# Two mixture stages: from all experts on all tokens to gathered rows of the chosen pairs

## The chip, the cores and the metric

The program runs on one core of one Trainium2 chip. The metric is the device time of one execution in microseconds (us), as the median of the runs. One execution was profiled; its rows are what the text argues from.

## The reference, cut to what matters

The program is six blocks on 4096 tokens of 256 numbers: a feed-forward block with 8 experts, an attention, that feed-forward block again, then a mixture block (stage d), a second attention (stage e) and the mixture block again (stage f). Only d and f are touched. Each computes

```python
scores = softmax(xt @ gate_w.T)          # 4096 x 16, xt is the normalised input
# only 2 of the 4 groups of 4 experts stay, and of what stays the best 4 experts
c = c.at[arange(T)[:, None], indices].add(weights)
h1 = einsum('td,edi->tei', xt, w1)       # 256 -> 128, 16 experts
h3 = einsum('td,edi->tei', xt, w3)
y = einsum('tei,eid,te->td', silu(h1) * h3, w2, c)   # 128 -> 256
z = silu(xt @ ws1) * (xt @ ws3) @ ws2    # two shared units of 128
x = x + 0.5 * (y + z)
```

A token uses 4 of 16 experts; the reference writes out all 16 with zero weights for the others.

## The kernel before

`moe` is called for d and f with the same code. A "unit" is one expert or one half of the shared network: 18 units. A "group" is 512 tokens (`GTOK`), so there are 8 groups (`NG`). The inputs are kept as two float32r parts, high and low, and each product is three matmuls (`mm3`, lines 60 to 62): high by high, high by low, low by high.

The stage loads x (`xs`), takes row statistics on VectorE (`row_stats`, line 70), normalises (line 924), transposes on TensorE (line 779), splits into `x_hi` on ScalarE (line 860) and `x_lo` on VectorE (line 931), and keeps both for the whole stage. Then it goes over units, and in each over the 8 groups. For one group and unit, TensorE runs `up` (12 matmuls of 512 columns into `h_ps`) and, for the group before, `down` (12 matmuls of 256 columns into `o_ps`); ScalarE takes the silu (line 868), VectorE multiplies (line 938), ScalarE copies the high part (line 874), GpSimd subtracts for the low part (line 903), and VectorE adds `coef * o_ps` into `xs` (line 954). `coef` is zero where a token did not choose the expert. The choice (`choose`, lines 965 to 1004) is cut into eight parts that VectorE does between the groups of unit 1. SP's queue loads each unit's weights ahead of time; the weight splits are lines 856 and 917. Units 2 to 15 run in a hardware loop (`Fori`).

Two other places are used for comparison. The routing in front of the 8-expert blocks (`ffn0_route`, stages ar and cr) has a loop on VectorE, lines 336 to 341, in which operands are indexed by the loop's counter, and builds one-hot rows (line 385) that TensorE multiplies (line 291). The experts of these blocks (stages ae and ce) gather rows with indirect DMAs from GpSimd's queue (line 484), and scatter with line 499.

Of the kernel before, what the change touches and what calls it, by code (L numbers as in the profile page):

```python
# [5 lines left out]
F32 = mybir.dt.float32  # L6
# [6 lines left out]
ds = bass.ds  # L13
# [665 lines left out]
UNITS = E1 + SHARED  # L679
INTER = 128  # L680
UCOL = 2 * KC * INTER + D


def moe(nc, tag, x_in, x_out, gate_w, w1, w3, w2, const):


    with ExitStack() as ctx:
        pool = Pools(nc, ctx, tag)
        sb, ps, sem = pool.sb, pool.ps, pool.sem
        xs = sb("xs", [P, NT, D])  # L690
        x_hi, x_lo = sb("x_hi", [P, KC, TOK], F32R), sb("x_lo", [P, KC, TOK], F32R)
        xn = sb("xn", [P, 2, GT, D])
        stats = sb("stats", [P, NT, 6])
        mean, var, rstd, tmp = (sb(n, [P, NT]) for n in ("mean", "var", "rstd", "tmp"))
        half = sb("half", [P, NT], I32)
        gw, gw_hi, gw_lo = sb("gw", [P, KC, E1]), sb("gw_hi", [P, KC, E1], F32R), sb("gw_lo", [P, KC, E1], F32R)
        coef, keep = sb("coef", [P, NT, 1 + E1]), sb("keep", [P, NT, E1])
        lg = sb("lg", [P, NT, E1])
        sc = sb("sc", [P, NT, E1])
        q = sb("q", [P, NT, E1])  # L700
        q2 = sb("q2", [P, NT, E1])
        pre = sb("pre", [P, NT, E1])
# [3 lines left out]
        raw = sb("raw", [P, 2, UCOL])  # L706
        w_hi, w_lo = sb("w_hi", [P, 2, UCOL], F32R), sb("w_lo", [P, 2, UCOL], F32R)
        s1, hid = sb("s1", [P, 2, GTOK]), sb("hid", [P, 2, GTOK])
        h_hi, h_lo = sb("h_hi", [P, 2, GTOK], F32R), sb("h_lo", [P, 2, GTOK], F32R)
        h1_ps, h3_ps = ps("h1_ps", [P, 2, 512]), ps("h3_ps", [P, 2, 512])  # L710
        o_ps = ps("o_ps", [P, 2, GT, D])

        loaded = [sem(f"loaded{g}") for g in range(NG)]
        c_loaded, own = sem("c_loaded"), sem("own")
        xn_ready, t_ready, x_hi_done, x_lo_done = (sem(n) for n in ("xn_ready", "t_ready", "x_hi_done", "x_lo_done"))
        gw_ready, lg_ready, lg_out, soft_in, soft_out = (sem(n) for n in ("gw_ready", "lg_ready", "lg_out", "soft_in", "soft_out"))
        w_in, w_hi_done, w_lo_done = [sem("w_in0"), sem("w_in1")], sem("w_hi_done"), sem("w_lo_done")
        h_ready, s1_ready, hid_ready, hid_hi, hid_lo = (sem(n) for n in ("h_ready", "s1_ready", "hid_ready", "hid_hi", "hid_lo"))
        o_ready, o_used, stored = sem("o_ready"), sem("o_used"), sem("stored")

        xv = x_in.rearrange("(t p) d -> p t d", p=P)
# [1634 lines left out]
```

## Time and profile before

| what | value |
|---|---|
| median of 3 runs | 4502.64 us (4502.56 to 4505.4) |
| the profiled execution, its own time | 4506.45 us |
| span of the profiled execution | 4504.7 us |
| TensorE busy in the span | 4003.0 us, 89% |
| stage d, from its first load to that of stage e | 1914.63 to 2603.50 us |
| stage f, from its first load to the end | 3815.8 to 4504.7 us |

The span runs from the first to the last instruction; 1.75 us of the execution's time lie around it. Busy time of TensorE counts matmuls that overlap, so the start of one matmul to the start of the next tells its cost better than its duration. Stage d and stage f have the same rows shifted in time, so only d is shown.

### The profile page before, as it was taken

Reading aid. Unit: us, or ns where it says so; the run is one execution under the profiler, and the core shown is the slowest. Engines: PE = TensorE matmul, PEld = TensorE weight load, DVE = VectorE, ACT = ScalarE, POOL = GpSimd, SP = SyncE. Lnnn points to the kernel's source line nnn. Section 1 sums busy time; section 2 is a strip of 40 time slices with the busy share of each in tenths; the row PEclk is TensorE's granted clock in tenths of the full one; section 3 lists DMA queues with packets and bytes.
Section 4 is the critical chain, followed back from the end, with each engine's and each line's share of the span. In section 5 each row is a group of like instructions: output and inputs, shape, how many; then the busy total and the mean of one; then the engine's idle time right before and its main releaser. Section 6 shows DMA issues by size and latency. Waiting matters only on the chain. (4 is left out here: it accounts for less than half of the span.)

```text
span 4504.7 us, 73929 instructions
## 1 busy us (share of the span) xinstructions
PE 4003.0 (89%) x26222; PEld 3087.4 (69%) x26222; DVE 2518.9 (56%) x4852; ACT 2003.3 (44%) x3837; POOL 956.5 (21%) x716
## 2 busy tenths in 40 slices
PE   4599959988974699879999969999999997899999
PEld 4499835555544599768888846666656664788888
DVE  4644346655645544356555546665666555565555
ACT  1566524444440666522333346555565554233332
POOL 0244312211200244313333300000000000133332
PEclk9999969999995799979999979999999999899999
DMA  3343210000003333210000010000000001000001
GB/s 116 94 102 78 35 53 15 15 21 16 25 26 102 117 82 80 33 52 15 10 11 14 24 61 1 11 10 11 1 11 10 11 6 41 20 11 10 14 10 38
DMA packets 144880, 159.27 MB, mean 35 GB/s; under 512 B 20320, under 2 KB 132704, under 8 KB 144352
## 3 DMA queue, kind: packets, MB, share of 16 engines
q1 hardware_dynamic: 117728, 113.15, 7.8%
q0 software_dynamic: 26880, 42.48, 5.0%
q8 instruction: 171, 2.80, 0.3%
q14 instruction: 101, 0.83, 0.1%
HBM read 105.01 MB, written 50.59 MB: 35 GB/s over the span
## 5 line engine op out<-in xcount | busy, mean ns | idle before, releaser
L1971 ACT ACTIVATE e_prob<-e_s_ps,e_small 128x512 f32<-128x512 f32 x512 | 346.7, 684 | 169.5 <-DVE e_small L2082 84.8
L2082 DVE TENSOR_REDUCE e_small<-e_s_ps 128x2 f32<-128x1024 f32 x256 | 313.2, 1223 | 168.3 <-PE e_s_ps L1848 164.3
L1388 ACT ACTIVATE b_pt<-b_t_ps 128x1024 f32<-128x1024 f32 (+3 forms) x256 | 180.8, 706 | 312.0 <-PE b_t_ps L1320 310.9
L903 POOL TENSOR_TENSOR f_h_lo<-f_hid,f_h_hi 128x512 fp32r<-128x512 f32 x144 | 188.2, 1307 | 518.2 <-ACT f_h_hi L874 518.2
L903 POOL TENSOR_TENSOR d_h_lo<-d_hid,d_h_hi 128x512 fp32r<-128x512 f32 x144 | 188.2, 1307 | 499.6 <-ACT d_h_hi L874 499.6
L2060 POOL TENSOR_TENSOR e_wide<-e_small,const 128x512 f32<-128x512 f32 x64 | 66.5, 1039 | 999.3 <-DVE e_small L2155 999.3
L1882 PE MATMUL e_z_ps<-e_pt,e_v 128*64 128x512 f32 x1024 | 275.5, 617 | 0.4 <-DVE e_zf L2162 0.4
L1861 PE MATMUL e_t_ps<-const,e_prob 128*128 128x128 f32 x2048 | 267.8, 274 | 6.1 <-ACT e_pt L1960 5.3
L1861 PEld LDWEIGHTS e_t_ps<-const,e_prob 128*128 128x128 f32 x2048 | 234.5, 141 | 51.1 <-issue 17.1
L1571 DVE TENSOR_REDUCE b_small<-b_s_ps 128x2 f32<-128x1024 f32 (+3 forms) x256 | 209.6, 819 | 84.7 <-PE b_s_ps L1299 80.7
L60 PE MATMUL d_h_ps<-d_x_hi,d_w_hi 128*128 128x512 f32 x576 | 231.0, 401 | 0.0
L60 PE MATMUL f_h_ps<-f_x_hi,f_w_hi 128*128 128x512 f32 x576 | 230.9, 401 | 0.0
L954 DVE SCALAR_TENSOR_TENSOR d_xs<-d_o_ps,d_coef,d_xs 128x256 f32<-128x256 f32 x516 | 214.0, 477 | 29.4 <-PE d_o_ps L62 26.8
L954 DVE SCALAR_TENSOR_TENSOR f_xs<-f_o_ps,f_coef,f_xs 128x256 f32<-128x256 f32 x516 | 214.0, 477 | 29.4 <-PE f_o_ps L62 26.7
L62 PE MATMUL f_h_ps<-f_x_hi,f_w_lo 128*128 128x512 f32 x576 | 230.3, 400 | 0.0
L62 PE MATMUL d_h_ps<-d_x_hi,d_w_lo 128*128 128x512 f32 x576 | 230.3, 400 | 0.0
L61 PE MATMUL d_h_ps<-d_x_lo,d_w_hi 128*128 128x512 f32 x576 | 229.5, 398 | 0.0
L61 PE MATMUL f_h_ps<-f_x_lo,f_w_hi 128*128 128x512 f32 x576 | 229.4, 398 | 0.0
L868 ACT ACTIVATE d_s<-d_h_ps 128x512 f32<-128x512 f32 x144 | 86.0, 597 | 315.6 <-PE d_h_ps L62 315.6
L868 ACT ACTIVATE f_s<-f_h_ps 128x512 f32<-128x512 f32 x144 | 86.0, 597 | 315.5 <-PE f_h_ps L62 315.5
L938 DVE TENSOR_TENSOR f_hid<-f_s,f_h_ps 128x512 f32<-128x512 f32 x144 | 99.0, 687 | 219.7 <-ACT f_s L868 219.2
L938 DVE TENSOR_TENSOR d_hid<-d_s,d_h_ps 128x512 f32<-128x512 f32 x144 | 99.0, 687 | 219.7 <-ACT d_s L868 219.1
(544 smaller groups left out, 11832.4 us busy)
## 6 DMA issues: line engine op xcount, KB each, us to landing
ae_raw<-w_dram SPq DMA_DIRECT2D x16, 1024.0 KB
ce_raw<-w_dram SPq DMA_DIRECT2D x16, 1024.0 KB
d_raw<-m_dram SPq DMA_DIRECT2D x54, 128.0 KB, 2.3
f_raw<-m_dram SPq DMA_DIRECT2D x54, 128.0 KB, 2.3
b_xs<-x_dram SPq DMA_DIRECT2D x9, 512.0 KB, 3.9
ar_xs<-x_dram SPq DMA_DIRECT2D x8, 512.0 KB, 9.2
x_dram<-ar_xs SPq DMA_DIRECT2D x8, 512.0 KB, 7.7
rows_dram<-ar_xn POOLq DMA_DIRECT2D x8, 512.0 KB
```

What stands on the lines that cost most here:

```text
L60: pe.matmul(out, a_hi, b_hi, start=start, stop=False, skip_group_check=True)
L61: pe.matmul(out, a_hi, b_lo, start=False, stop=False, skip_group_check=True)
L62: return pe.matmul(out, a_lo, b_hi, start=False, stop=stop, skip_group_check=True)
L903: gp.tensor_tensor(h_lo[:, g % 2], hid[:, g % 2], h_hi[:, g % 2].bitcast(F32), ALU.subtract).then_inc(hid_lo, 1)
L938: dve.tensor_tensor(hid[:, g % 2], s1[:, g % 2], h3_ps[:, g % 2], ALU.mult).then_inc(hid_ready, 1)
L954: last = dve.scalar_tensor_tensor(xs[:, tile], o_ps[:, 0 if head else g % 2, t], c, xs[:, tile], ALU.mult, ALU.add)
L1388: act.activation(pt[:, kt % 2, a, :, 0:width], t_ps[:, :, 0:width], ACT.Exp).then_inc(p_ready, 1)
L1571: dve.tensor_reduce(nm[:, o % 2, qt, 2 * a:2 * a + 2], s_ps[:, :, 0:(qt + 1) * P], AX.X, ALU.max, negate=True).then_inc(mx_ready, 1)
L1861: last = pe.transpose(t_ps[:, h, kt * P:(kt + 1) * P], prob[:, bank_of(s) + h, kt * P:(kt + 1) * P], ident)
L1882: last = pe.matmul(z_ps[rows, 0], v[:, pr // 4, kt, c:c + DK1], pt[:, buf, h, kt], start=(kt == 0), stop=(kt == QT - 1), skip_group_check= ...
L1971: act.activation(prob[:, at], s_ps[:, at], ACT.Exp, bias=nmx[:, at:at + 1], accum_out=sums[:, buf, h * QT + s:h * QT + s + 1]).then_inc(p_ ...
L2082: dve.tensor_reduce(nmx[:, at:at + 2], s_ps[:, at:at + 2], AX.X, ALU.max, negate=True).then_inc(mx_ready, 1)
```

## The change

Both calls of `moe` are replaced by one of this order. The input is normalised in place, and the normalised rows are stored to DRAM (`xn_rows`). The logits are computed with the gate weights as stationary operand (high and low in one) and turned back. `choose` runs in one piece. `places` gives each of the 16384 token and expert pairs a place in a list sorted by expert, in which each expert starts on a new tile of 128 rows: at most 144 tiles (`COLS`). `lists` builds the list of token numbers with one-hot rows on VectorE and 128 small matmuls. `owners` works out which expert owns each tile, and packs eight owners in a 32-bit word.

Then come 72 steps of two tiles, with 4 more to drain. GpSimd gathers the two tiles' rows; TensorE turns them, multiplies them as stationary operand by the owner's w1 and w3 (256 columns), turns the hidden rows, and multiplies by w2. The column at which the expert's weights begin is worked out on TensorE's queue from the word, for each tile. The results are stored to DRAM (`o_rows`) in the list's order. At the end the two shared units run over 8 groups of tokens, while GpSimd gathers four rows for each token (128 indirect DMAs), and VectorE adds them, weighted, to x.

The core of the diff (lines left out are marked):

```diff
+COLS, BODY = 144, 8
+TWO, TURN = 2, BODY // 2
+TILE_STEPS = COLS // TWO
...
+        def over_steps(eng, step, begin=None):
...
+            with eng.Fori(2, TILE_STEPS // TURN) as i:
+                first = begin(i) if begin else None
+                for u in range(TURN):
+                    step(i * TURN + u, u, first)
...
+            # on GpSimd
+            for j in range(COLS):
+                if j >= BODY and j % TWO == 0:
+                    gp.wait_ge(t_ready, j // TWO - TURN + 1)
+                gp.indirect_dma_start(out=xg[:, j % BODY], out_offset=None, in_=xn_rows,
+                                      in_offset=bass.IndirectOffsetOnAxis(ap=token_i[:, j:j + 1], axis=0)).then_inc(
+                                          gathered[j // TWO % TURN], 16)
+            for part in range(2):
+                gp.wait_ge(stored[part], 16 * (COLS // BODY))
+            for t in range(NT):
+                if t >= TAKE and t % GT == 0:
+                    gp.wait_ge(used, (t - TAKE) // GT + 1)
+                for k in range(TOPK):
+                    gp.indirect_dma_start(out=takes[:, t % TAKE, k], out_offset=None, in_=o_rows,
+                                          in_offset=bass.IndirectOffsetOnAxis(ap=back[:, t, k:k + 1], axis=0)).then_inc(taken[t % TAKE], 16)
...
+            # on TensorE
+            def begin(i):
+                return [pe.value_load(words[0:1, at(i + n)]) for n in range(2)]
+            def offset(packed, n):
+                return ((packed >> (28 - 4 * n)) & 15) * UCOL
+            def step(j, u, packed):
+                if within(j, 0):
+                    pe.wait_ge(gathered[u], (j - u) * 8 + 32)
+                    if past(j, 2):
+                        pe.wait_ge(x_lo_done, j - 1)
+                    for n in range(TWO):
+                        for k in range(KC):
+                            c = n * D + k * P
+                            last = pe.transpose(pa[:, u % 2, c:c + P], xg[:, TWO * u + n, k * P:(k + 1) * P], ident)
+                    last.then_inc(t_ready, 1)
...
+                if within(j, 1):
+                    m, s = j - 1, (u - 1) % TURN
+                    pe.wait_ge(x_lo_done, m + 1)
...
+                    for n in range(TWO):
+                        up_at = offset(packed[0], 6 + n) if u == 0 else offset(packed[1], TWO * (u - 1) + n)
+                        for k in range(KC):
+                            c = n * D + k * P
+                            last = mm3(pe, ph[:, s % 2, n * HCOL:(n + 1) * HCOL], x_step(xh, s)[:, c:c + P], x_step(xl, s)[:, c:c + P],
+                                       w_hi[:, ds(up_at + k * HCOL, HCOL)], w_lo[:, ds(up_at + k * HCOL, HCOL)], k == 0, k == KC - 1)
...
+            # on VectorE
+            def lists():
+                for t in range(NT):
+                    if t >= 3:
+                        dve.wait_ge(hot_used, t - 2)
+                    dve.tensor_tensor(hot_row[:, t % 3], iota_b[:, 0:P].unsqueeze(1).to_broadcast([P, TOPK, P]),
+                                      row[:, t].unsqueeze(2).to_broadcast([P, TOPK, P]), ALU.is_equal)
+                    for k in range(TOPK):
+                        last = dve.tensor_scalar(hot_col[:, t % 3, k], iota_b[:], col[:, t, k:k + 1], ids_i[:, t:t + 1].bitcast(F32),
+                                                 ALU.is_equal, ALU.mult)
+                    last.then_inc(hot_ready, 1)
...
+            def collect(g):
+                dve.wait_ge(zo_ready, g + 1)
+                dve.wait_ge(xs_in[g % 2], 16 * (g // 2 + 1))
+                for t in range(GT):
+                    part = po[:].rearrange("p b (t d) -> p (b t) d", d=D)[:, t]
+                    last = dve.scalar_tensor_tensor(xr[:, g % 2, t], part, 0.5, xr[:, g % 2, t], ALU.mult, ALU.add)
+                last.then_inc(zo_used, 1)
+                dve.wait_ge(zo_used, g + 1)
+                for k in range(TOPK):
+                    for t in range(GT):
+                        n = g * GT + t
+                        if k == 0:
+                            dve.wait_ge(taken[n % TAKE], 16 * TOPK * (n // TAKE + 1))
+                        last = dve.scalar_tensor_tensor(xr[:, g % 2, t], takes[:, n % TAKE, k], coef[:, n, k:k + 1], xr[:, g % 2, t],
+                                                        ALU.mult, ALU.add)
```

In a step, every engine does a different stage of different tiles: in step j TensorE turns the rows of step j, turns the hidden rows of step j-3, runs `up` for step j-1 and `down` for step j-4. ScalarE copies the high part of the turned rows (512 wide), takes the silu (256), copies the hidden rows' high part (256), and every second step copies the result (512). VectorE does the low parts (512 and 256), the product (256) and the other results (512).

## Rows read from the trace of the kernel before

**Rows 1.** The page's head and its list of busy time by engine

```profile
span 4504.7 us, 73929 instructions
PE 4003.0 (89%) x26222; PEld 3087.4 (69%) x26222; DVE 2518.9 (56%) x4852; ACT 2003.3 (44%) x3837; POOL 956.5 (21%) x716
```

**Rows 2.** Busy time by stretch, stage d, in the order PE, PEld, DVE, ACT, POOL, clock

```profile
1914.00:1960.00 46.00, 16.92 (x85) 15.14 (x86) 24.71 (x77) 6.46 (x10) 1.27 (x1) 0.56 0.38 117
2090.00:2580.00 490.00, 490.00 (x2791) 428.80 (x2790) 284.50 (x594) 153.34 (x247) 151.94 (x116) 1.00 0.04 12
```

**Rows 3.** Timeline of TensorE inside the units of stage d: start, duration, instruction

```profile
2300.14 0.40 PE L60 MATMUL d_h_ps<-d_x_hi,d_w_hi 128*128 128x512 f32 x1
2300.38 0.40 PE L61 MATMUL d_h_ps<-d_x_lo,d_w_hi 128*128 128x512 f32 x1
...
2300.84 0.28 PE L60 MATMUL d_o_ps<-d_w_hi,d_h_hi 128*128 128x256 f32 x1
...
2302.27 0.39 PE L60 MATMUL d_h_ps<-d_x_hi,d_w_hi 128*128 128x512 f32 x1
```

**Rows 4.** Timeline of stage d's two ends, all engines

```profile
1914.63 0.38 SPq L757 DMA_DIRECT2D d_xs<-x_dram  x1
...
1919.04 1.40 DVE L70 BATCH_NORM_STATS2 d_small<-d_xs 128x6 f32<-128x256 f32 x4
...
1953.07 0.63 PE L60 MATMUL d_h_ps<-d_x_hi,d_w_hi 128*128 128x512 f32 x1
1953.50 0.63 PE L61 MATMUL d_h_ps<-d_x_lo,d_w_hi 128*128 128x512 f32 x1
...
2599.59 0.36 SPq L768 DMA_DIRECT2D x_dram<-d_xs  x1
2603.50 0.36 SPq L1791 DMA_DIRECT2D e_xs<-x_dram  x1
```

**Rows 5.** Groups by line and shape, stage d: busy us, mean ns of one

```profile
L860 ACT ACTIVATE d_x_hi<-d_o_ps 128x512 fp32r<-128x512 f32 x16 | 9.5, 592 | 43.5 <-PE d_o_ps L779 43.5
L931 DVE TENSOR_TENSOR d_x_lo<-d_o_ps,d_x_hi 128x512 fp32r<-128x512 f32 x16 | 11.0, 687 | 21.4 <-ACT d_x_hi L860 21.4
L988 DVE MAX8 d_small<-d_q 128x8 f32<-128x16 f32 x32 | 2.5, 156 | 0.0
L1001 DVE SCALAR_TENSOR_TENSOR d_pre<-d_pre,d_q 128x512 f32<-128x512 f32 x1 | 1.3, 1340 | 0.0
L999 DVE TENSOR_TENSOR d_pre<-d_pre,d_small 128x512 f32<-128x512 f32 x1 | 0.7, 691 | 0.0
```

**Rows 6.** Timeline of VectorE around one line-954 block, stage d

```profile
2293.23 0.69 DVE L938 TENSOR_TENSOR d_hid<-d_s,d_h_ps 128x512 f32<-128x512 f32 x1 [1.65 <-ACT d_s L868]
2294.14 1.66 DVE L954 SCALAR_TENSOR_TENSOR d_xs<-d_o_ps,d_coef,d_xs 128x256 f32<-128x256 f32 x4 [0.22 <-PE d_o_ps L62]
2297.45 0.69 DVE L938 TENSOR_TENSOR d_hid<-d_s,d_h_ps 128x512 f32<-128x512 f32 x1 [1.65 <-ACT d_s L868]
```

**Rows 7.** Timeline of VectorE building one-hot rows, stage ar

```profile
133.57 5.76 DVE L385 TENSOR_TENSOR ar_hot_r<-ar_iota_b,ar_row_b 128x1024 bf16<-128x1024 bf16 x5
```

**Rows 8.** Timeline of GpSimd and TensorE: gathers and turned rows, stages ce and ar

```profile
1507.12 1.00 POOL L484 DMA_INDIRECT ce_xg<-rows_dram,c_idx  x1 [0.31 <-issue]
1508.42 0.95 POOL L484 DMA_INDIRECT ce_xg<-rows_dram,c_idx  x1 [0.30 <-issue]
1509.67 0.94 POOL L484 DMA_INDIRECT ce_xg<-rows_dram,c_idx  x1 [0.30 <-issue]
...
1513.44 1.11 PE L520 MATMUL ce_t_ps<-const,ce_xg 128*128 128x128 f32 x4 [9.88 <-DMA ce_xg<-rows_dram,c_idx]
...
1904.35 1.55 POOL L499 DMA_INDIRECT x_dram<-ce_y,c_idx  x1 [0.30 <-issue]
```

**Rows 9.** Timeline of TensorE: eight turned tiles in stage ar, four in stage d

```profile
39.35 1.95 PE L247 MATMUL ar_tp<-const,ar_xn 128*128 128x128 f32 x8
...
1955.95 0.60 PE L779 MATMUL d_o_ps<-const,d_xn 128*128 128x128 f32 x4
```

**Rows 10.** Timeline of VectorE in the routing loop and just behind it, stage ar

```profile
74.99 0.22 DVE L340 SCALAR_TENSOR_TENSOR ar_small<-ar_small 128x1 f32<-128x1 f32 x1 [0.17 <-DVE ar_small L339]
75.35 0.22 DVE L341 SCALAR_TENSOR_TENSOR ar_small<-const,ar_small 128x3 f32<-128x3 f32 x1
76.03 0.48 DVE L336 TENSOR_SCALAR_CACHE_REDUCE ar_small<-ar_small 128x256 f32<-128x256 f32 x1 [0.46 <-DVE ar_small L341]
...
118.38 0.21 DVE L344 TENSOR_SCALAR ar_small<-ar_small 128x1 f32<-128x1 f32 x1 [0.21 <-DVE ar_small L341]
118.63 0.35 DVE L345 TENSOR_SCALAR ar_small<-ar_small 128x256 f32<-128x256 f32 x1
```

**Rows 11.** Timeline of TensorE: small matmuls of the routing, stage ar

```profile
140.75 0.36 PE L291 MATMUL ar_idp<-ar_ids,ar_hot_a 128*128 128x16 bf16 x8
```

More of the change, by code:

```diff
@@ L733, in w2_of @@
[L733 to L746 removed]
+        xs = big[:].rearrange("p (t d) -> p t d", d=D)
@@ new lines, in logits @@
+            def logits(g):
+                pe.wait_ge(a_lo_done, (g + 1) * KC)
+                if g >= 2:
+                    pe.wait_ge(lg_out, g - 1)
+                for k in range(KC):
+                    for n, part in enumerate((xh, xl)):
+                        last = pe.matmul(ph[:, g % 2], gw_hl[:, k], x_group(part)[:, g % 2, k], start=(k + n == 0),
+                                         stop=(k == KC - 1 and n == 1), skip_group_check=True)
+                last.then_inc(lg_ready, 1)
@@ L895, in _, with copy @@
-            unit(1, NG, 1, True)
-            over_units(act, unit)
-        @block.gpsimd
-        def _(gp):
-            def unit(b, first, u, more):
-                for g in range(NG):
-                    gp.wait_ge(hid_hi, first + (g + 1))
-                    gp.tensor_tensor(h_lo[:, g % 2], hid[:, g % 2], h_hi[:, g % 2].bitcast(F32), ALU.subtract).then_inc(hid_lo, 1)
-            unit(0, 0, 0, True)
-            unit(1, NG, 1, True)
-            over_units(gp, unit)
+            def copy(out, in_, ready):
+                act.activation(out, in_, ACT.Copy).then_inc(ready, 1)
@@ new lines, in _ @@
+            for h in range(2):
+                roots(h)
+                dve.wait_ge(norm_ready, h + 1)
+                norm(h)
+            for g in range(NG):
+                for k in range(KC):
+                    split(g, k, a_hi_done, turned_in[g % 2], a_lo_done)
+            for u in range(BY_POOL, E1 - 2):
+                low(u)
+            choose()
+            for u in range(E1 - 2, E1):
+                low(u)
+            places()
+            lists()
+            owners()
+            over_steps(dve, step)
@@ L1010, in _ @@
+            for u in range(E1, E1 + SHARED):
+                low(u)
             for k in range(KC):
[L1011 removed]
+                split(0, k, zx_hi, pa, zx_lo)
+            factors()
             for g in range(NG):
+                z_mult(g, 0)
                 if g + 1 < NG:
[L1014 to L1020 removed]
@@ L1022, in unit @@
-            def unit(b, first, u, more):
-                for g in range(NG):
-                    step(b, g, first, u + 1 if more else None)
-                    if g >= 1:
-                        add(g - 1, first, u)
-                    else:
-                        add(NG - 1, first - NG, u - 1)
-                    if isinstance(u, int) and u == 1:
-                        choose(g)
-            unit(1, NG, 1, True)
-            over_units(dve, unit)
-            add(NG - 1, (UNITS - 1) * NG, UNITS - 1)
+                    split(g + 1, 0, zx_hi, pa, zx_lo)
```

784 lines of the change are left out of this document (530 added, 254 removed).

## The prediction

> **What bounds the kernel now.** I read the page's head first, then the busy time by stretch, then timelines inside stage d. TensorE is busy for 4003 of 4504.7 us [rows 1]. In stage d it is busy without a gap for all of 490 us, at clock 1.00 [rows 2]. So the matmuls are the bound, and only fewer or cheaper ones shorten the stage. The reader should see the pace in the timeline: a 512-column matmul follows the last after 0.24 us, and the 12 of 256 columns take 2300.84 to 2302.27, 0.119 us each [rows 3]. One group of one unit needs 12 x 0.232 + 12 x 0.119 = 4.2 us, and VectorE's product indeed returns every 4.22 us [rows 6]. 18 units x 8 groups x 4.22 = 608 us. The stage lasts from 1914.6 to 2603.5, 688.9 us [rows 4]; of it some 46 us at the front leave TensorE mostly idle [rows 2]. Two such stages are 1378 us.
>
> **What is removed.** 16 of the 18 units on all tokens: 16 x 8 x 4.22 = 540 us a stage. The shared two remain but move to the end.
>
> **What is added: the path before the steps.** The choice was hidden between groups; it now has nothing beside it. I take it stage by stage, from the first load.
> - To the logits. Load to first statistics 4.4 us [rows 4]. The second half of the rows is ready after 32 statistics at 0.35 and two short chains: some 27 us in. Six groups then go at TensorE's slow pace: 8 turned tiles 8 x 0.217 (1.95 us for eight, the last overlapping) [rows 9], four 512-column matmuls at 0.43 [rows 4], the turning back: 4.3 us if slow, 3.5 if ScalarE's copies of 0.59 [rows 5] set it. I take 51 us in all.
> - `choose`: 20 operations on 512 numbers at 0.69 us, three at 1.34 and 32 maxima (2.5 us) [rows 5], with the exponential's round trip: 23 us.
> - `places` with two weight splits and two matmuls in front: 14 us from the same rows.
> - `lists`: 32 times one comparison of 512 and four of 144. The nearest row is 1024 numbers in 1.15 us [rows 7], so 0.6 + 4 x 0.17 = 1.3 us; 32 make 41 us. Bounds 35 to 50. TensorE's part hides under it: 8 bf16 pairs took 0.36 us [rows 11].
> - First tiles: two gathers issued, then landing. The first turned rows came 6.3 us after the second gather's start [rows 8], with other loads in flight. I take 5.
> Together 51 + 23 + 14 + 41 + 5 = 134 us. The weight splits and the storing of normalised rows cost nothing: ScalarE, GpSimd and SP's queue do them under the normalising, and three raw buffers keep them ahead; without that cover they would be some 5 us.
>
> **The steps.** A step has 18 matmuls of 256 columns and 6 turned tiles. At full clock 18 x 0.119 + 6 x 0.11 (four in 0.60, the last 0.27 of it overlapping) = 2.8 us [rows 3, 9]. GpSimd's two gathers are 2 x 1.25 = 2.5 us [rows 8], hidden by that. ScalarE has 0.59 + 2 x 0.38 + 0.3 = 1.7 us, VectorE 0.69 + 2 x 0.42 + 0.35 = 1.9 us [rows 5]; both hide. No operation of a step is needed by TensorE in the same step, so the engines' waits do not add up. The store of four tiles is one issue on SP's queue each second step.
>
> But TensorE's queue must also work out addresses, and this kernel has no such matmul. The nearest row is VectorE's routing loop: lines 340 and 341, indexed by the counter, start 0.36 us apart, where lines 344 and 345, with fixed places, start 0.25 apart [rows 10]: 0.11 us for each value worked out. Going round the loop costs 0.46 - 0.17 = 0.3 us more [rows 10]. How many values does a step need? For each tile, unpacking the owner and one address for each different weight slice: at least 1 + 4 for `up`, 1 + 2 for `down`, 16 a step. If each of the 9 moving operands has its own, and unpacking takes two, 26; with eight waits on counted values, 34. I take 20 and count four waits that cannot be folded: 24 x 0.11 = 2.6 us. The queue must also pass 24 weight loads and matmuls; the fastest pairs go at 0.36 / 8 = 0.045, or some 0.027 between starts [rows 11]: 0.65 us. The loop and the two words read are shared by four steps: I take 0.5 a step. 2.6 + 0.65 + 0.5 = 3.8 us. This is more than the 2.8 of matmuls, so **I expect TensorE's queue, not its array, to set the step: 3.8 us**. Bounds: 2.8 if the queue's work hides, 5.5 if 34 values are needed and matmuls with such an address pass more slowly. 76 steps x 3.8 = 289 us.
>
> The words' reading is shown by no row. The Trainium skill, "DMA: Bandwidth & Descriptors", section "Latency and other measured facts", gives a `tensor_load` a floor of some 600 ns. By that page, two for four steps would be an estimated 0.3 us a step, or 23 us a stage; no trace here has one.
>
> **The end.** The last results must be stored before the first is gathered back: 3 us, as the next stage's load starts 3.9 us after the last store's issue [rows 4]. GpSimd then issues 128 gathers, 128 x 1.25 = 160 us. Under them: TensorE's shared units, 8 x 2 x 4.22 plus turning, 75 us; VectorE per group 20 weighted adds at 0.395 (1.66 for four) [rows 6] and six of 0.69, 12 us against GpSimd's 20. So GpSimd's queue sets this part. After its last gather: landing 3, 20 adds 7, store 3: 13 us. Together 3 + 160 + 13 = 176 us. A gather cannot be below 1.25 by any row; if it costs what the scatters do, 1.85 [rows 8], the part grows by 77 us.
>
> **Sum.** 134 + 289 + 176 = 599 us against 689: 90 us less, twice, 180 us. 4506.5 - 180 = 4326 for the profiled execution; the median lies 3.8 us below it, so 4323 us.
>
> **The rivals.**
> - A, above: the step is set by TensorE's queue, 3.3 to 4.8 us, giving 4247 to 4475. For it: the routing loop's rows. Against it: on VectorE each operation waits for the one before; TensorE's queue may run ahead. Chance 0.53.
> - B: the queue's work hides under matmuls, step 2.9: 134 + 220 + 176 = 530, 2 x 159 less: 4185 us. For it: in stage d matmuls follow each other without gap although its loop has counted waits too [rows 2]. Chance 0.18.
> - C, the other side: one mechanism, dear addresses. Step 5.5: 134 + 418 + 176 = 728: 39 more, twice: 4581 us. It decides from a step of (689 - 310) / 76 = 5.0 us. For it: 34 values at 0.11 are 3.7 alone. Chance 0.17.
> - D, other side too: TensorE's pauses bring the clock to 1.2 GHz. The same 512 columns took 0.43 instead of 0.24 us [rows 4, 3], a turned tile 0.217: a step 18 x 0.215 + 6 x 0.217 = 5.2 us, 705 us a stage: 4535 us. For it: the front of stage d had clock 0.56 [rows 2]. Against it: 2.8 of 3.8 us are busy. Chance 0.07.
> - E: VectorE keeps GpSimd from writing its gathers. If half an operation of 0.69 (0.35 to 0.5) comes on top of each, the end is 128 x 1.73 = 221 instead of 160 us and the steps stay under 3.8: 660 a stage: 4445 us. Against it: beside VectorE's subtractions in stage ce the gathers kept 1.25 us [rows 8]. Chance 0.05. The Trainium skill, "SBUF — State Buffer", section "Who interferes with whom", states that descriptor writing by GpSimd is fully blocked while VectorE runs a two-port copy. By that page the copies of results, which read PSUM here, would have to fall under it; by the rows of the sum they don't.
>
> **How the numbers follow.** The prediction is A's, 4323. The range goes from B's end, 4190, to 4560, which takes in D and a part of C; about 2 in 10 lie outside. The likeliest case's own range is 4247 to 4475. Faster: A, B and E less a little, 0.74. Within 0.2% (9 us, about what can be told from no change): steps within 0.06 us of 5.0, 0.03. Slower: C and D, 0.23.
>
> **What would show it.** Steps: `up`'s matmuls return every 3.8 us, with pauses put down to issue and not to another engine; at 2.9 B is right, above 5.0 C. The clock row in the steps tells D. `lists` lasts 41 us on VectorE. The gathers of the end start 1.25 us apart and set the last third. The prediction is wrong if a step waits for gathers or for ScalarE, or if the path before the steps is far from 134 us.

## The result and the profile after

The changed kernel takes 4263.33 us (median of 4 runs, 4260.56 to 4265.76) against 4503.79 (4502.56 to 4505.4): ratio 0.9463, 95% interval 0.9452 to 0.9474, 240 us less. The prediction was 4323 in a range from 4190 to 4560, for the case that TensorE's queue sets the step at 3.3 to 4.8 us.

The experiments brought out one thing that belongs here. On a later occasion the same kernel, unchanged, took 4412.55 us (4401.45 to 4427.67) beside 4503.79 for the kernel before: ratio 0.9797, interval 0.9768 to 0.9826. The kernel before does not change from one occasion to the other; the changed one does, by 3.5%. The record gives the later occasions' chips, a different one each time, but not the result's. Unless it is said otherwise, "after" is the kernel of the result.

The head of the page of after; the instructions of TensorE have fallen from 4003 us to 3416 [rows 1]:

```profile
span 4264.0 us, 70943 instructions
PE 3415.9 (80%) x23666; PEld 2590.7 (61%) x23669; DVE 2408.5 (56%) x4776; ACT 1941.6 (46%) x3904; POOL 1167.7 (27%) x1012
```

Busy time in stage d by stretch (as in [rows 2]): front, choosing and places, lists, first gathers, steps, end.

```profile
1910.00:1967.00 57.00, 24.01 (x113) 18.47 (x113) 33.88 (x103) 26.91 (x48) 25.32 (x17) 0.61 0.70 208
1967.00:2011.00 44.00, 3.53 (x19) 2.01 (x19) 31.70 (x119) 8.54 (x11) 6.13 (x4) 0.55 0.29 84
2011.00:2061.00 50.00, 21.16 (x128) 11.87 (x128) 49.18 (x165) 0.00 (x0) 0.00 (x0) 0.50 0.00 1
2061.00:2067.00 6.00, 0.00 (x0) 0.00 (x0) 1.58 (x7) 0.00 (x0) 3.95 (x4) 0.50 0.73 240
2067.00:2295.00 228.00, 215.65 (x1734) 209.28 (x1735) 124.24 (x252) 110.24 (x254) 132.40 (x140) 0.99 0.55 165
2295.00:2475.00 180.00, 93.02 (x444) 78.63 (x442) 108.46 (x224) 28.51 (x50) 125.41 (x128) 0.74 0.51 157
```

The columns are time, busy TensorE, its weight loads, VectorE, ScalarE, GpSimd, granted clock, share and rate of the DMA engines. The bound moves from engine to engine: VectorE alone in the lists (49.18 of 50 us), TensorE in the steps (215.65 of 228, clock 0.99), GpSimd in the end (125.41 of 180 busy, and the 0.30 behind each gather). The stage lasts from the first load, 1910.04, to the next stage's, 2475.37: 565.3 us against 688.9 [rows 4]. Stage f is as long, and twice 123.6 is 247.2 us; the rest of the span grew by 6.5 us (stage d starts 4.6 us earlier, the work between the two stages is 11 longer).

The path ahead of the steps, timeline of VectorE:

```profile
1977.83 0.96 DVE L1324 TENSOR_TENSOR d_w_lo<-d_raw,d_w_hi 128x768 fp32r<-128x768 f32 x1 [10.14 <-ACT d_w_hi L1059]
1979.51 0.96 DVE L1324 TENSOR_TENSOR d_w_lo<-d_raw,d_w_hi 128x768 fp32r<-128x768 f32 x1 [0.73 <-ACT d_w_hi L1059]
1980.39 0.68 DVE L1205 COPY d_big<-d_pt 128x512 f32<-128x512 f32 x1
...
2021.62 0.68 DVE L1275 TENSOR_TENSOR d_xg<-d_iota_b,d_small 128x512 bf16<-128x512 bf16 x1
2022.22 0.99 DVE L1278 TENSOR_SCALAR d_xg<-d_iota_b,d_small 128x144 bf16<-128x144 bf16 x4
2023.13 0.68 DVE L1275 TENSOR_TENSOR d_xg<-d_iota_b,d_small 128x512 bf16<-128x512 bf16 x1
```

VectorE idles 10.14 us in front of a weight's low part that stands in its queue before `choose` (L1205), and a tile of the lists takes 1.51 us (2021.62 to 2023.13). Some of the 10.14 us is a wait for the logits, as an experiment below shows. They are late themselves because ScalarE's queue has a weight's high part in front of its last copy of logits, and waits for that weight's load:

```profile
1970.92 0.84 ACT L1059 ACTIVATE d_w_hi<-d_raw 128x768 fp32r<-128x768 f32 x1 [3.25 <-DMA d_raw<-m_dram]
...
1972.29 0.63 PE L930 MATMUL d_pt<-const,d_hid 32*128 32x32 f32 x4 [3.00 <-ACT d_hid L1059]
```

A step on TensorE; the last line is the first of the next round of the loop:

```profile
2149.74 0.28 PE L60 MATMUL d_ph<-d_w_hi,d_xh 128*128 x1
2149.86 0.28 PE L61 MATMUL d_ph<-d_w_lo,d_xh 128*128 x1
...
2150.70 0.28 PE L62 MATMUL d_po<-d_w_hi,d_hl 128*128 x1
2151.61 0.65 PE L949 MATMUL d_pa<-const,d_xg 128*128 128x128 f32 x4 [0.64 <-issue]
```

Matmuls with a worked-out address follow each other every 0.12 us, as the plain ones of before [rows 3]. Only once in four steps is there a hole, 0.9 us from start to start, put down to no engine. TensorE's queue has records of its own (PEldq) there, by line from 2150 to 2152 us: the loop's branch and the reads of two words.

```profile
L786 PEldq COMPARE_BRANCH  x1: 208/208/208, 2150.2 to 2150.2; - x1
L936 PEldq TENSOR_LOAD <-d_small x2: 299/302/306, 2150.6 to 2151.1; - x2
```

From the start of the branch to that of the first register operation behind the reads, at 2151.42, are 1.2 us, or 0.3 a step.

The end of the stage, timelines of GpSimd, VectorE and SyncE's queue:

```profile
2461.03 0.95 POOL L900 DMA_INDIRECT d_w_hi<-o_rows_dram,d_small  x1 [0.30 <-issue]
2462.28 0.95 POOL L900 DMA_INDIRECT d_w_hi<-o_rows_dram,d_small  x1 [0.30 <-issue]
...
2465.09 5.61 DVE L1364 SCALAR_TENSOR_TENSOR d_big<-d_w_hi,d_small,d_big 128x256 f32<-128x256 f32 x13 [4.59 <-DMA d_w_hi<-o_rows_dram,d_small]
...
2470.73 0.36 SPq L865 DMA_DIRECT2D x_dram<-d_big  x1
2475.37 0.36 SPq L2170 DMA_DIRECT2D e_xs<-x_dram  x1
```

The gathers go to their last at 1.25 us each (1.29 in the mean of all 128), then 2.8 us of landing, 5.6 of adds, 4.6 of store: the tail that the prediction had at 13 us.

### The profile page after: what moved, and what is told of

Read it like the earlier page. It is cut to its first block and busy times, and to the rows that moved or that the text cites. A ratio compares the mean times of both kernels' runs of the same rounds, so it can differ in the third digit from the quotient of the medians.

```text
span 4264.0 us, 70943 instructions
## 1 busy us (share of the span) xinstructions
PE 3415.9 (80%) x23666; PEld 2590.7 (61%) x23669; DVE 2408.5 (56%) x4776; ACT 1941.6 (46%) x3904; POOL 1167.7 (27%) x1012
## 3 DMA queue, kind: packets, MB, share of 16 engines
q1 hardware_dynamic: 153440, 176.07, 12.6%
## 5 line engine op out<-in xcount | busy, mean ns | idle before, releaser
L2467 DVE COPY e_pt<-e_t_ps 128x512 f32<-128x512 f32 x256 | 175.2, 684 | 71.8 <-PE e_t_ps L2240 67.2
L891 POOL DMA_INDIRECT d_xg<-xn_rows_dram,d_small x144 | 136.3, 947 | 161.8 <-DVE d_small L1284 84.7
L891 POOL DMA_INDIRECT f_xg<-xn_rows_dram,f_small x144 | 136.2, 946 | 161.7 <-DVE f_small L1284 84.8
L1673 PE MATMUL b_s_ps<-b_k_all,b_q_all 64*128 64x256 f32 (+3 forms) x512 | 110.2, 427 | 58.7 <-DVE b_small L1950 51.7
L499 POOL DMA_INDIRECT x_dram<-ae_y,a_idx x64 | 103.7, 1621 | 189.9 <-ACT ae_y L585 175.3
L499 POOL DMA_INDIRECT x_dram<-ce_y,c_idx x64 | 103.7, 1620 | 189.8 <-ACT ce_y L585 175.2
L2339 ACT ACTIVATE e_pt<-e_t_ps 128x512 f32<-128x512 f32 x256 | 153.8, 601 | 2.2 <-PE e_t_ps L2240 2.2
L62 PE MATMUL ce_o_ps<-ce_w_hi,ce_h_lo 128*128 128x256 f32 x512 | 144.9, 283 | 0.0
L62 PE MATMUL ae_o_ps<-ae_w_hi,ae_h_lo 128*128 128x256 f32 x512 | 144.9, 283 | 0.0
L61 PE MATMUL ae_o_ps<-ae_w_lo,ae_h_hi 128*128 128x256 f32 x512 | 144.8, 283 | 0.0
```

The lines of the kernel that those rows point to most:

```text
L61: pe.matmul(out, a_hi, b_lo, start=False, stop=False, skip_group_check=True)
L62: return pe.matmul(out, a_lo, b_hi, start=False, stop=stop, skip_group_check=True)
L499: gp.indirect_dma_start(out=x_out, out_offset=bass.IndirectOffsetOnAxis(ap=idx[:, e, c:c + 1], axis=0), in_=y[:, g, t], in_offset=None, co ...
L891: gp.indirect_dma_start(out=xg[:, j % BODY], out_offset=None, in_=xn_rows, in_offset=bass.IndirectOffsetOnAxis(ap=token_i[:, j:j + 1], axi ...
L2467: dve.tensor_copy(pt[:, buf, 1, :, s * P:(s + 1) * P], t_ps[:, 1].rearrange("p (k q) -> p k q", k=QT)).then_inc(pt_dve, 1)
```

## The experiments

Three theories on the step: Q, TensorE's queue (addresses) sets it; M, the array's matmuls; G, GpSimd's gathers, next at 2.5 us. Two on the rest: the waits of the front, and GpSimd's gathers as the end's bound. The kernels ran on four occasions: the first four, the next four, the control with one more, and the last two; those of one occasion ran beside each other, on chips 6, 5, 15 and 1 in turn. Where no interval is given, a time is that of a single execution.

**Fixed addresses.**

```diff
             def offset(packed, n):
-                return ((packed >> (28 - 4 * n)) & 15) * UCOL
+                return 0
```

> The kernel after, with every tile's weights taken at a fixed address (expert 0's), so TensorE works out no offset; the two words are still read once in four steps. Left out: the choice of the expert, so the mixture is computed with one expert's weights; the instructions of all other engines are the same. Steps of the changed kernel take 3.0 us (228 us for 76), of which the array's matmuls hold 2.84. Theory Q (the address work sets the step, about 24 values and waits of 0.11 us in 2.75 us): the queue falls below 1 us, the array alone is left at 2.84 plus the word reads' gap, so at most -12 us a stage. Theory M (the array sets the step and the address work is hidden in it): 228 us a stage stays within 3 us. The whole kernel: 4240 to 4250 by Q, 4258 to 4264 by M.

Measured: 4407 us. TensorE's queue has no read of a word in this run. All that line 936 left there, in both stages, is the wait ahead of the first read:

```profile
L936 PEldq EVENT_SEMAPHORE  x2: 51/51/51, 2056.1 to 3918.3; - x2
```

So the reads went out with the offsets that used them, and on TensorE's queue this kernel and the next differ by hardly anything.

**Fixed addresses, no words read.** `begin` returns constants as well.

> As the kernel with fixed addresses, and the words are not read either (nothing chooses the expert). One gap of 0.9 us of TensorE in each iteration of four steps is a branch and two reads of 0.30 us. If the reads make the gap, it falls by some 0.6 us in 18 iterations and the two ends: -12 us a stage, -24 in all against the run with fixed addresses. If the branch makes it, nothing moves.

Measured: 4392 us.

**Two products.** The steps call this instead of `mm3`:

```diff
+def mm2(pe, out, a_hi, a_lo, b_hi, b_lo, start, stop):
+    pe.matmul(out, a_hi, b_hi, start=start, stop=False, skip_group_check=True)
+    return pe.matmul(out, a_hi, b_lo, start=False, stop=stop, skip_group_check=True)
```

Here `a` are the activations and `b` the weights.

> The kernel after, with the third product (low part of the activations times high part of the weights) left out of the steps' matmuls: 6 of 18 matmuls of 256 columns less a step, 0.71 us of the array; the addresses are worked out as before. Left out: that part of the result. Theory Q: the queue's 2.75 us and the words stand, the step stays at 2.95 to 3.0 and the stage's steps at 224 to 228 us. Theory M: the array falls to 2.13, the step to GpSimd's two gathers of 1.25 = 2.5 us, 190 us a stage: -76 us over both stages, 4187.

Measured: 4425 us.

**Both.**

> Fixed addresses, no word reads and two products: neither address work nor the array is left to set the step (left out: the choice of expert and the third product). Both theories: GpSimd's gathers bind at 2 x 1.25 = 2.5 us, 190 us for 76 steps, 4187. If it goes lower than 2.5 the gathers overlap better than their spacing says; if it stays at 3.0, something else than TensorE sets the step (ScalarE's or VectorE's chain through the buffers).

Measured: 4385 us.

**More register work.**

```diff
-                return ((packed >> (28 - 4 * n)) & 15) * UCOL
+                return (((((packed >> (28 - 4 * n)) >> 0) & 127) & 15) * UCOL)
```

> The kernel after with one register operation more in each of a step's four weight offsets (nothing else changes, the result is the same). At 0.11 us each TensorE's queue takes 0.44 us more a step. Theory Q (queue sets the step): the step goes from 3.0 to 3.4, +33 us a stage, 4330. Theory M with the queue and the array almost level (2.75 and 2.84): the first 0.1 is covered, +0.35 a step, +27 us a stage, 4315. If the queue has real slack under the array: nothing, 4263.

Measured: 4478 us.

**Half of the rows gathered back.**

```diff
-                for k in range(TOPK):
+                for k in range(TOPK // 2):
                     gp.indirect_dma_start(out=takes[:, t % TAKE, k], out_offset=None, in_=o_rows,
...
```

VectorE waits for two rows of a token and takes each of them twice.

> The kernel after, gathering two of the four result rows of each token at the end (the two are added twice; left out: the other two experts' results). If GpSimd's 128 gathers of 1.25 us set the last 180 us of a stage, 64 of them take 80 us and the end falls until TensorE's shared units (93 us busy) or VectorE (108 us busy) bind: 115 to 130 us instead of 180, some -100 to -130 over both stages, 4135 to 4165. If the shared units' own chain sets the end (as VectorE's instructions between the waits might): under -30, above 4230.

Measured: 4197 us.

**Choosing first.**

```diff
-            for u in range(BY_POOL, E1 - 2):
-                low(u)
             choose()
-            for u in range(E1 - 2, E1):
+            for u in range(BY_POOL, E1 - 2):
                 low(u)
             places()
             lists()
+            for u in range(E1 - 2, E1):
+                low(u)
```

On ScalarE the exponential stands behind the weights up to 11 instead of 13.

> The kernel after with an order that lets the choice of experts pass the weights: VectorE chooses first and makes the low parts of experts 12 and 13 behind it, those of 14 and 15 behind the lists; ScalarE takes the exponential ahead of the weights 12 and 13. Theory S (the wait of 10.1 us ahead of the choice is on the path): choosing starts 8 us earlier, the stage ends 8 us earlier, -16 us in all, 4247, ratio to before 0.943. Rival: the weights come later then and the first step waits for them, so that the end does not move, 4263.

Measured: 4389.93 us (4388.76 to 4392.45), ratio to before 0.975 (0.9734 to 0.9767).

**A third of the row comparisons on GpSimd.**

```diff
+            for t in range(2, NT, 3):
+                if t >= 3:
+                    gp.wait_ge(hot_used, t - 2)
+                for k in range(TOPK):
+                    last = gp.tensor_scalar(hot_row[:, t % 3, k], iota_b[:, 0:P], row[:, t, k:k + 1], None, ALU.is_equal)
+                last.then_inc(row_by_pool, 1)
...
```

VectorE leaves these rows out, and TensorE waits for GpSimd as well.

> The kernel after with the row comparison of every third tile of the lists on GpSimd (four instructions of 128 columns instead of one of 512 on VectorE, 10 of 32 tiles). VectorE's work in the lists falls from 49 to about 42.5 us. Theory P (VectorE alone sets this stretch and GpSimd runs free beside it): -6 us a stage if GpSimd's four take less than 4 us, -13 in all, 4250. Rival (the two engines hold each other up, or GpSimd's small instructions are dear): VectorE's own instructions lengthen or TensorE waits for GpSimd, no gain or a loss, 4263 or more.

Measured: 4382 us.

Seven of the eight lie some 120 to 200 us above the highest time that a theory gave (most of all the one with both edits, 4385 for 4187). No edit could explain that: two of them only shorten the front. So the kernel itself came next, beside one without gathers.

**The control**, no edit, and **the steps without their gathers**:

```diff
-            for j in range(COLS):
+            for j in range(BODY):
...
-                    pe.wait_ge(gathered[u], (j - u) * 8 + 32)
+                    if not past(j, TURN):
+                        pe.wait_ge(gathered[u], (j - u) * 8 + 32)
```

The second part also takes a wait, and the value that it counts up to, out of TensorE's queue.

> The changed kernel once more, with no edit. Seven edited kernels gave 4382 to 4478 where 4187 to 4330 was expected; in their traces TensorE's semaphores are raised late while GpSimd gathers (VectorE and ScalarE idle beside finished matmuls). Theory C (late semaphores belong to the conditions of a run, not to the edits): this run shows them too, about 217 us instead of 213 between a stage's first and last y copy, about 230 instead of 177 to the last store, and some 4385. Theory E (each of the edits brought them in, and the order or count of instructions decides): this run gives 4263 again.

Measured: 4412.55 us (4401.45 to 4427.67), ratio 0.9797 (0.9768 to 0.9826). Theory C holds: the extra time is in the unchanged kernel too.

> The changed kernel with only the first 8 of 144 gathers of the steps, and no wait for the others: the same eight columns of tokens are worked through again and again (left out: all other tokens' rows). TensorE, ScalarE and VectorE do the same work in the steps and GpSimd none. If GpSimd's gathers hold TensorE's semaphores up or set the step: the step falls below the 3.0 us of the other run of this call, to the array's 2.84 or the queue's 2.75 plus 0.2. If TensorE alone sets the step and the late semaphores are hidden behind it: 213 to 217 us between the first and the last y copy as before, no gain in the steps.

Measured: 4376 us, and 204.6 us between the first and the last y copy, against 217.2 of the control.

What is late is seen in the control's end. Timelines of TensorE, ScalarE and GpSimd in one group of the shared units:

```profile
2331.71 1.04 PE L988 MATMUL d_pa<-const,d_xg 128*128 128x128 f32 x8
2332.50 0.36 PE L60 MATMUL d_po<-d_w_hi,d_hh 128*128 128x256 f32 x1
...
2335.33 0.28 PE L62 MATMUL d_po<-d_w_hi,d_hl 128*128 128x256 f32 x1
2359.91 0.80 PE L60 MATMUL d_ph<-d_xh,d_w_hi 128*128 128x512 f32 x1 [24.30 <-DVE d_xl L1329]
...
2334.45 0.60 ACT L1059 ACTIVATE d_xh<-d_pa 128x512 fp32r<-128x512 f32 x1 [4.68 <-remote]
2340.07 0.60 ACT L1059 ACTIVATE d_xh<-d_pa 128x512 fp32r<-128x512 f32 x1 [5.03 <-remote]
2357.11 0.63 ACT L1059 ACTIVATE d_hh<-d_hid 128x512 fp32r<-128x512 f32 x1 [16.44 <-remote]
...
2351.45 0.95 POOL L900 DMA_INDIRECT d_w_hi<-o_rows_dram,d_small  x1 [0.30 <-issue]
2369.07 0.94 POOL L900 DMA_INDIRECT d_w_hi<-o_rows_dram,d_small  x1 [16.68 <-DVE d_big L1364]
```

The eight turned tiles are done by 2332.8; ScalarE waits for nothing but TensorE's semaphores, and copies them at 2334.45 and 2340.07. The last matmul for d_po ends at 2335.6; ScalarE's copy to d_hh, which waits for its semaphore, starts at 2357.11, 21.5 us later. It is released only when GpSimd has run out of room (32 gathers are out, the last at 2351.45) and stands still. "remote" is the trace's word for a wait that it can give to no record. The same place in after:

```profile
2333.97 1.09 ACT L1059 ACTIVATE d_xh<-d_pa 128x512 fp32r<-128x512 f32 x2 [2.58 <-PE d_pa L988]
2337.34 0.63 ACT L1059 ACTIVATE d_hh<-d_hid 128x512 fp32r<-128x512 f32 x1 [2.27 <-PE d_po L62]
```

There the gathers run without a pause as well, and no semaphore is late. All the experiments' profiled executions have late ones; only that of the result has none.

One more difference stands in the traces, and it leaves a rival to everything below that calls a gather the cause. Both executions have 70943 instructions of the same program, but the trace of after holds 30850 semaphore events and that of the control 21084. The difference begins before anything changed: from 163 to 572 us, where 8-expert blocks run as in the kernel before, after has 3362 events, the control 2466, and the kernel before 2482. So the trace of every kernel with late semaphores lacks a part of these events; that of the kernel before does too, and its time stays the same. Each gather raises its semaphore by 16, so gathers, the landing of their data, and the recording of these events come together. That the lateness goes with gathers is shown; which of the three holds TensorE up is not, nor whether it would be there without recording. With pauses between gathers (below), where the lateness is smaller, the trace holds 23422 events; in all others with late semaphores it is 20656 to 21716.

The last two kernels test this reading, and the two edits of the front together. **Two orders**: the edits of choosing first and of the comparisons on GpSimd. **Pauses**: the same, with

```diff
                                           in_offset=bass.IndirectOffsetOnAxis(ap=back[:, t, k:k + 1], axis=0)).then_inc(taken[t % TAKE], 16)
+                    if k % 2:
+                        gp.wait_ge(idled, 2 * t + k // 2)
+                        gp.tensor_scalar(idle_o[:], ident[:, 0:64], 1.0, None, ALU.mult).then_inc(idled, 1)
```

> The changed kernel with two earlier edits together: the choice of experts passes the weights' low parts, and the row comparison of every third tile of the lists is on GpSimd. Measured one by one, from the first statistics to the first gather: 140.5 and 142.6 us against 146.9 and 148.2 in two runs without them. Together the first gather should come 10 to 11 us earlier in each stage. If TensorE's semaphores are raised late in this run, as in the last control (4412): 4390; if they are on time, as in the run of the result (4263): 4242. A time above 4405 would say that the front is won and given back before the steps.

Measured: 4388.82 us (4378.02 to 4402.96), ratio 0.9753 (0.9722 to 0.9784).

> As the kernel with the two orders, and after every second of the 128 gathers at a stage's end GpSimd does one small instruction of about 0.5 us, so that two gathers take about 3.1 us instead of 2.5. Theory L (gathers issued one after another hold up the semaphores of TensorE by up to 21 us, small gaps let them through, as in the steps where they are late by about 1 us): GpSimd's 64 pairs take 198 us, the stage's end (last y copy to last store) falls from 232 to 244 us to about 210, -50 to -60 in all against the kernel without pauses. Rival (what delays them is the number of gathers outstanding or the shared units' own traffic): the end stays at 230 or grows. Where the semaphores are on time in this run, the end grows from 177 to about 212 instead.

Measured: 4320.92 us (4314.23 to 4326.56), ratio 0.9593 (0.957 to 0.9616). 68 us less than without pauses, on the same occasion; 50 to 60 were expected.

The parts of stage d, from each trace. Front: first statistics to first gather. Fill: to the first y copy on ScalarE. Steps: to its last, 35 of 36 copies later, which is 70 steps. End: to the last store. Stage f agrees within 2.2 us in front, fill and steps; where its end differs by more, it stands behind the stroke.

| kernel | front | fill | steps | a step | end |
|---|---|---|---|---|---|
| after | 147.4 | 18.5 | 213.1 | 3.04 | 177.2 |
| control | 148.2 | 26.6 | 217.2 | 3.10 | 243.4 |
| fixed addresses | 146.9 | 25.9 | 211.3 | 3.02 | 244.2 |
| ... and no words | 147.4 | 25.9 | 211.5 | 3.02 | 243.9 / 233.1 |
| two products | 148.2 | 24.6 | 227.6 | 3.25 | 232.0 / 244.6 |
| both | 148.3 | 25.1 | 206.8 | 2.95 | 232.9 / 245.0 |
| more register work | 146.3 | 26.6 | 234.3 | 3.35 | 243.3 |
| half gathered back | 146.9 | 26.4 | 217.0 | 3.10 | 133.0 |
| choosing first | 140.5 | 25.8 | 218.4 | 3.12 | 231.3 / 243.4 |
| comparisons on GpSimd | 142.6 | 26.1 | 216.8 | 3.10 | 232.2 |
| steps without gathers | 147.2 | 18.3 | 204.6 | 2.92 | 239.7 / 231.9 |
| two orders | 136.0 | 26.5 | 217.3 | 3.10 | 233.5 |
| pauses | 135.6 | 26.1 | 217.8 | 3.11 | 204.3 |

The rows behind the steps' column (group of ScalarE's y copies) for after and without gathers:

```profile
L1101 ACT ACTIVATE d_big<-d_po x36: 597/599/602, 2080.4 to 2293.5; 128x512 f32<-128x512 f32 x36
```

```profile
L1102 ACT ACTIVATE d_big<-d_po x36: 598/598/601, 2090.3 to 2294.9; 128x512 f32<-128x512 f32 x36
```

What follows, one by one.

- **The control against after**: +8 fill, +4 steps, +66 end in stage d, twice: 156 us, against 149 between the medians and 154 between the two profiled executions. Late semaphores cost most where GpSimd gathers without a pause beside a chain that passes from engine to engine.
- **The lateness goes with the gathers.** Without them the fill falls by 8 us to after's value, beside the control, and the steps by 12.6 us. Of these 12.6 some 7 can be the wait that this edit also took out of TensorE's queue (0.1 us a step, see the queue below). With half of the gathers back the end is 133 us instead of 243; with pauses 204. The idle time of the instructions on d_hh in the end that no record explains (us, times), first two orders, then pauses:

```profile
  remote: 74.6, 4
```

```profile
  remote: 5.8, 1
```

  The pause itself, timeline of GpSimd:

```profile
2329.60 0.97 POOL L909 DMA_INDIRECT d_w_hi<-o_rows_dram,d_small  x1 [0.31 <-issue]
2330.60 0.39 POOL L913 TENSOR_SCALAR d_small<-const 128x64 f32<-128x64 f32 x1
2331.16 0.98 POOL L909 DMA_INDIRECT d_w_hi<-o_rows_dram,d_small  x1 [0.17 <-issue]
2332.45 0.97 POOL L909 DMA_INDIRECT d_w_hi<-o_rows_dram,d_small  x1 [0.31 <-issue]
```

  A pair takes 2.85 us here instead of 2.5. GpSimd issues more slowly and the stage is done 29 us earlier (233.5 - 204.3); its last gather starts 196 us behind the last y copy instead of 207, because it stands still less. Both ends together are 56 of the 59 us between the two profiled executions.
- **The queue against the array.** The matmuls of a step fill 2.84 us of the array in every one of these kernels but those with two products. The step moves with the records on TensorE's queue (register operations, waits, reads and the branch): counted from the first to the last y copy 24.1 a step without gathers and 2.92 us, 25.1 and 3.04 in after, 28.4 and 3.35 with more register work. That is 0.10 us for each, and in after's queue two register operations with nothing between them start 0.10 us apart (2153.47, 2153.56, 2153.66). So in after the queue most likely sets the step (Q), though only by 0.2 us over the array. Doubts stay: the kernel without gathers lacks more than queue records, the kernel with more register work ran with late semaphores and that of after did not, and the control, with 24.9 records, has 3.10 us, 0.08 above this line.
- **Fixed addresses** take the queue down to 5.9 records, and the hole of each round goes from 0.9 us to nothing. The step is 3.02 us all the same, because TensorE now waits for VectorE's low part of the hidden rows:

```profile
2151.11 0.39 PE L60 MATMUL d_po<-d_w_hi,d_hh 128*128 128x256 f32 x1 [0.84 <-DVE d_hl L1313]
```

  In this run TensorE's semaphores reach ScalarE late in the steps too (52 us of idle time that no record explains in 170), and that chain sets the step, as its waits have it. What fixed addresses would give with semaphores on time, 2.84 us by Q and M alike, no run shows.
- **The number of values.** Groups of TensorE's queue in 180 us (59 steps) of after:

```profile
L60 PEldq ALU_OP  x396: 36/36/36, 2105.1 to 2284.9; - x198
L60 PEldq FUSED_REGOPS  x348: 46/51/60, 2105.3 to 2284.1; - x174
L61 PEldq ALU_OP  x348: 32/36/36, 2105.4 to 2284.2; - x174
```

  1092 / 59 = 18.5 a step. With the waits' own values and the loop's share it is 21, and 3.4 waits, where the prediction took 20 and four.
- **The words.** The two kernels with fixed addresses (211.3 and 211.5 us) don't test their reading, since neither reads them. That the reads and the branch make the hole is read from the queue's records in after, and fits that the hole is gone without them. Of the 16 us between the two kernels' times 10 lie in the ends, which differ by as much between the stages of one execution.
- **Two products** did not shorten the step but lengthened it, 3.25 us, against both theories. Its trace shows TensorE waiting up to 2.05 us a round, and the clock at its lower level behind that (0.53 granted from 2154 to 2157 us, 0.95 in the steps as a whole):

```profile
2151.57 0.28 PE L67 MATMUL d_po<-d_w_lo,d_hh 128*128 x1
2153.90 1.11 PE L954 MATMUL d_pa<-const,d_xg 128*128 128x128 f32 x4 [2.05 <-issue]
...
2155.66 0.41 PE L66 MATMUL d_ph<-d_w_hi,d_xh 128*128 x1
2155.88 0.41 PE L67 MATMUL d_ph<-d_w_lo,d_xh 128*128 x1
```

  0.21 us between starts instead of 0.12 is the level of 1.2 GHz. It is not only semaphores that are late here: register operations on TensorE's queue, which wait for nothing, last up to 0.7 us, where those in after's steps last at most 0.06.

```profile
L66 PEldq FUSED_REGOPS  x325: 3/46/698, 2105.1 to 2284.2; - x163
```

  With both edits the step is 2.95, not the 2.5 of GpSimd's gathers. With the array out of the way, late semaphores and these dips seem to set the step; that is argued from the rows, not shown by a run.
- **The end** is GpSimd's: with half of its gathers it is 110 us shorter. 64 gathers less are 80 us of issuing; the other 30 are put down to lateness by subtraction alone. In after, where nothing is late, that GpSimd sets the end is read from its timeline and not from a run.
- **The front.** Choosing first brings the first gather 7 us closer to the first statistics and GpSimd's comparisons 4 to 5 us; together 12 of 148, each as expected. The whole kernel's time can't show them: 4389.93 with the one, 4382 with the other, 4388.82 with both and 4412.55 for the control, on three occasions, with ends that vary by 12 us. VectorE's copy that begins `choose`, with choosing first:

```profile
1973.06 0.69 DVE L1205 COPY d_big<-d_pt 128x512 f32<-128x512 f32 x1 [5.05 <-PE d_pt L930]
```

  It waits for the logits now, not for a weight, and starts at 1973.06 instead of 1980.39, in a stage that begins at the same 1910.0: of the 10.14 us, up to 1973.06 were the logits' (5.4) and 4.8 the weights'. With the 2.6 us from the start of the first low part to `choose`, the weights cost 7.3 in all. Beside VectorE, which keeps its 0.68 us, GpSimd's 40 comparisons take 774 ns each, four for a tile 3.1 us:

```profile
L893 POOL TENSOR_SCALAR d_xg<-d_iota_b,d_small 128x128 bf16<-128x128 bf16 x40 | 30.4, 774 | 44.4 <-DVE d_small L1278 34.2 <-PE d_po L1045 10.2
```

Not tried: the version with pauses where semaphores are on time. There the pauses should cost, since the end of after (177) is already shorter than theirs (204). It beats the kernel before in every run and the changed kernel in late ones; it is not shown to beat the changed kernel of the result.

## Why the prediction was right, and where it was not

The sum was 134 + 289 + 176 = 599 us for a stage, and 565 came: 157 + 228 + 180. The miss of 60 us in the whole is one term too low and one too high.

1. **Before the steps, 157 instead of 134.** To the logits 63 instead of 51 (1910.0 to 1973.06, read where nothing else stands in VectorE's way): the first of the last six groups is turned 33 us in and not 27, each takes 4.4 us as TensorE waits for GpSimd's normalised tile (by up to 2.78 us), and the last logits come 3 us late behind a weight. `lists` 50 instead of 41, at the upper bound, because the four small comparisons take 0.99 us and not 0.68. The step that failed outright is "The weight splits and the storing of normalised rows cost nothing": the three raw buffers did not keep the splits ahead. Two low parts in VectorE's queue ahead of `choose` cost 7.3 us and a high part in ScalarE's 3 us, where the prediction had some 5 without the cover. `choose` took 19 us (1980.4 to 1999.5) instead of 23, splits and `places` 11.5 instead of 14, the first tiles 6 instead of 5. By the prediction's own sign, a path "far from 134 us", this part was missed by a sixth.
2. **The steps, 228 instead of 289.** That TensorE's queue sets the step was right, as far as the runs show it; so were the price of a value (0.10 us for 0.11) and the number (21 values and 3.4 waits for 20 and 4). The step that failed is "The queue must also pass 24 weight loads and matmuls", 0.65 us, added on top: 24 x 0.11 and the 0.3 for branch and words make 2.9, and the step is 3.04, so hardly anything is left for them. The queue hands over matmuls while it works out addresses. The 0.5 for loop and words was 0.3. So the step fell between rivals A (3.3 at least) and B (2.9), nearer to B's, though not by B's mechanism alone. "The queue, not its array" holds by 3.04 against 2.84 only.
3. **The end, 180 instead of 176.** GpSimd's queue sets it: 164 us from its first gather to the end of the last one's issue, where 160 was predicted, and a tail of 13 us (2.8, 5.6 and 4.6 for 3, 7 and 3).
4. **C** (dear addresses) is out: matmuls with such an address start every 0.12 us. **D** did not come in after, clock 0.99 in the steps; with two products it shows in places. **E**, GpSimd's writing held up by VectorE, is out: gathers stay at 1.25 us beside VectorE's copies and adds. The Trainium skill, "SBUF — State Buffer", section "Who interferes with whom", has a VectorE operation in a two-port mode block GpSimd, and says that copies can enter one; the trace shows no such hold-up here.
5. **What no rival held**: TensorE's semaphores late while GpSimd gathers, 150 us in the whole kernel on another occasion. The range covers 4412 too, but by other mechanisms. And it is luck that the miss is 60 us and not 120: before the steps 23 us a stage were lost, in the steps 61 won.

The read of a word on TensorE's queue took 0.30 us in this trace (36 reads, 297 to 312 ns in stage f), half of the floor of some 600 ns that the Trainium skill states in "DMA: Bandwidth & Descriptors", section "Latency and other measured facts"; the measurement decides. The estimate of 0.3 us a step from that page was too high for the reads alone, which take 0.15; branch and reads together are 0.3.

```profile
L936 PEldq TENSOR_LOAD <-f_small x36: 297/303/312, 3851.9 to 4075.7; - x36
```

## What to carry to other kernels

When a kernel trades matmuls for gathers, count an engine's queue and its array as two lines that run side by side, and take the larger, not their sum: 24 values and waits at 0.11 us, with 0.3 for loop and words, gave 2.9 beside 2.84 of matmuls, and the step was 3.04. Look for a wait that stands in an in-order queue ahead of the critical work. Where GpSimd gathers beside a chain that goes from engine to engine, measure the unchanged kernel again together with every experiment: here the same program differed by 149 us between two occasions. And ask whether an edit took out more than it names: fixed addresses took out the reads, and a missing gather took out its wait. Where semaphores are late, a small pause between gathers can end the stage earlier than gathering at full pace (204 us instead of 233).

## What was not expected of the hardware

- In all traces of the changed kernel and its variants but that of the result TensorE's semaphores reach ScalarE and VectorE late while GpSimd issues indirect DMAs: by up to 21.5 us in the group shown, at 1.25 us a gather, while semaphores of VectorE and ScalarE come in time there. An instruction of 0.39 us after each pair brings the unexplained idle time around d_hh from 74.6 us to 5.8 in a stage's end. The same traces hold a third fewer semaphore events than that of after. What differs between the occasions (chips among it), whether recording has a part in it, and why only TensorE is hit, stays open.
- A dynamic address costs TensorE's matmuls nothing on the array: 0.12 us between starts with it as without it. Its queue pays 0.10 us for each register operation or wait, beside the matmuls and not on top of them.
